# A twelve-stage decoder kernel: the scan stage interleaved over its token groups, with its last norm and the context attention's first queries moved across the stage border

## The reference

```
fg  = sigmoid(h @ W_F)                                  # (tokens, 128)
t   = h @ W_toP + sum_i W_V[:, i] * (h @ W_U[:, :, i])  # four products, i = 0..3
lam = sigmoid(fg @ W_lam);  u = t @ B_mat               # (tokens, 64)
s_n = lam_n * s_(n-1) + u_n                             # a scan along each sequence
x   = x + (t + s @ C_mat) @ W_fromP
```

## Time and profile before

| | |
|---|---|
| median of 3 runs | 2536.81 us (2535.66 to 2538.05) |
| the profiled execution | 2539.63 us |
| its span in the trace | 2537.8 us |
| busy in the span | PE 80%, DVE 58%, ACT 43%, POOL 29% |
| scan stage in the trace | 970.8 to 1066.0 us |
| first score matmul of the context attention | 1075.2 us |

### The profile page before, as it was taken

The page is one execution under the profiler, slowest core; times in us unless marked ns, Lnnn a source line. Parts: engine busy times, 40 slices in busy tenths (PEclk is TensorE's granted clock), DMA queues, the critical chain, the costliest instruction groups (busy, mean ns, idle before and its releaser), DMA issues.

```text
span 2537.8 us, 34717 instructions
## 1 busy us (share of the span) xinstructions
PE 2033.2 (80%) x12069; PEld 1385.2 (55%) x12069; DVE 1482.4 (58%) x4604; ACT 1087.6 (43%) x2654; POOL 748.3 (29%) x755
## 2 busy tenths in 40 slices
PE   4778776989799997488872999857778887998779
PEld 3444444777555563255631678646645456666546
DVE  5655535444475555378740386488767764666662
ACT  2232232544443331078710256667657322666331
POOL 3111123211132230124236155364343332001252
PEclk9899988999899998789975999978989898999789
DMA  2000000200330001100043145600040000000000
GB/s 95 1 0 34 0 34 2 87 26 1 140 118 1 1 1 65 42 18 27 10 175 120 49 138 154 202 1 1 1 169 22 30 1 15 1 1 2 36 1 34
DMA packets 39117, 117.52 MB, mean 46 GB/s; under 512 B 6672, under 2 KB 24208, under 8 KB 36848
## 3 DMA queue, kind: packets, MB, share of 16 engines
q1 hardware_dynamic: 31312, 94.19, 11.1%
q0 software_dynamic: 7632, 21.11, 2.2%
HBM read 92.08 MB, written 36.04 MB: 50 GB/s over the span
## 4 chain that ended last, share of the span: by engine, by line
PE 58%; DVE 18%; ACT 11%; POOL 5%; issue 4%; another core or an unknown queue 3%; DMA 1%; POOLq 0%; DVEq 0%; SPq 0%; ACTq 0%
PE ps L215 37%; PE ps L737 5%; ACT BIG L814 3%; PE ps L709 3%; PE ps L756 3%; PE ps L1771 2%; PE ps L280 2%; DVE XN L271 1%; ACT BIG L290 1%; DVE SML L256 1%; PE ps L1783 1%; PE ps L843 1%; PE ps L1247 1%; POOL SML L221 1%
## 5 line engine op out<-in xcount | busy, mean ns | idle before, releaser
L215 PE MATMUL ps<-BIG 128*128 128x256 f16 (+2 forms) x1616 | 341.7, 361 | 26.4 <-DVE BIG L2339 12.9
L814 ACT ACTIVATE BIG<-BIG,SML 128x256 f32<-128x256 f32 (+1 forms) x768 | 302.5, 483 | 23.8 <-DVE SML L777 23.8
L215 PEld LDWEIGHTS ps<-BIG 128*128 128x128 f16 (+1 forms) x1616 | 223.9, 140 | 121.6 <-issue 66.6
L737 PE MATMUL ps<-CST,BIG 128*128 128x128 f32 x1408 | 217.0, 290 | 41.8 <-ACT BIG L814 26.1
L635 POOL TENSOR_TENSOR BIG<-BIG 128x512 f16<-128x512 f32 x120 | 142.2, 1186 | 293.2 <-ACT BIG L569 264.9
L737 PEld LDWEIGHTS ps<-CST,BIG 128*128 128x128 f32 x1408 | 160.9, 146 | 118.7 <-ACT BIG L814 76.6
L215 PE MATMUL ps<-XN,BIG 128*128 128x512 f16 x864 | 206.8, 396 | 13.8 <-ACT BIG L546 4.9
L219 POOL TENSOR_SCALAR SML<-SML 128x4 f32<-128x4 f32 (+1 forms) x88 | 24.4, 277 | 640.6 <-DVE SML L259 267.7
L777 DVE CUSTOM_DVE_ANT_0 BIG<-ps,BIG 128x256 f32<-128x256 f32 x512 | 181.3, 420 | 51.1 <-PE ps L709 50.6
L290 ACT ACTIVATE BIG<-ps 128x512 f32<-128x512 f32 (+1 forms) x240 | 126.7, 564 | 145.9 <-PE ps L737 108.5
L215 PE MATMUL ps<-XT,WA 128*128 128x256 f32 (+1 forms) x320 | 123.6, 523 | 65.7 <-ACT XN L1988 27.1
(11 more groups left out here) (391 smaller groups left out, 4057.3 us busy)
## 6 DMA issues: line engine op xcount, KB each, us to landing
slots<-in_zeros SPq DMA_DIRECT2D x19, 660.0 KB, 24.0
WA<-slots SPq DMA_DIRECT2D x95, 132.0 KB
BIG<-in_l1e SPq DMA_DIRECT2D x2, 4224.0 KB, 17.2
BIG<-spread SPq DMA_DIRECT2D x16, 512.0 KB, 6.1
BIG<-in_l0e SPq DMA_DIRECT2D x8, 768.0 KB, 7.8
BIG<-in_ctxT SPq DMA_DIRECT2D x8, 512.0 KB, 3.6
BIG<-in_ctxT SPq DMA_DIRECT2D x16, 256.0 KB, 3.1
BIG<-in_ctx SPq DMA_DIRECT2D x16, 256.0 KB, 3.6
```

The costliest lines, as they stand in the source:

```text
L215: m = T.e.matmul(ps, l, r, start=i == 0, stop=i == len(pairs) - 1)
L737: m = T.e.transpose(PS[r][:, o:o + P], c["SM"][n % 2 * 4 + i][:, q, tok(k)], ident)
L814: A.e.activation(s[:, q, 0:kn[q]], s[:, q, 0:kn[q]], ACT.Exp, bias=mx[:, q:q + 1], scale=-1.0).then_inc(*(A.sig("exp", p, n, i) if q else ...
```

## The change

The scan stage is interleaved. PE runs the products of group g with `cs(g-1)` put before the second `up`, the transposes of group g-2 before the third, and `fp(g-1)` between `lam(g)` and `ui(g)`. DVE starts a round with the scan of g-1, and the scaling and copy of group g-2's norm come between its additions; the statistics of g-1 end the round. ACT's and POOL's lists follow. The norm of the last group (3) leaves the scan stage: its statistics, root, scaling, transposes and copies are side work of the context attention, at steps 6, 14 and 16 there and, on POOL, after the mask of the fourth sequence.

The loads of `itok` and of the first two sequences' keys and values are issued at the beginning of the scan stage, ahead of the expert weights that SP loads there. POOL sets the columns of ones, converts `itok`, and makes the queries, mask and values of the first sequence inside the scan stage. For this the scan stage's tiles tT and lam move to the end of RING and ui, sT, FG and TT to the upper part of SCR, and the attention's VA, KB, VR, AM and QB lie in the lower part. The other context attention (phase 7) uses the same functions and keeps its order.

The diff, cut to its core:

```diff
-            return p in (2, 8, 11) and p != phases[0] and g == NG - 1
+            return p in (2, 4, 8, 11) and p != phases[0] and g == NG - 1
...
                     norm_upper(after(p), b // 2)
 
+        def late_dve(p):
+
+            if ends_later(p, NG - 1):
+                norm_stats(p, NG - 1)
+                yield from pause(14)
+                norm_scale(V, p, NG - 1)
+                yield from pause(4)
...
+
+        def late_pe(c):
+            if ends_later(c["p"], NG - 1):
+                yield from pause(18)
...
+        def late_act(p):
+            if ends_later(p, NG - 1):
+                yield from pause(18)
+                norm_copy(A, p, NG - 1, 0)
...
+        def first_kv(c):
             if c["p"] == 4:
                 SP.e.dma_start(c["sq"], a["itok"]).then_inc(*SP.sig("itok", by=16))
...
+            for b in range(2):
+                load_kv(c, b)
+
+        def ctx_sp(c):
+            if c["p"] != 4 or 3 not in phases:
+                first_kv(c)
...
+                waits(G, ("xt", 4, b // 2, 0), ("xt", 4, b // 2, 1))
...
-        def ctx_pool(c):
+        def ctx_ready_pool(c):
             p = c["p"]
             ones_columns(c)
             waits(G, (f"w{p}",), ("ones", p, 0), ("ones", p, 1))
...
-            ctx_mask_pool(c, 0)
...
+        def ctx_pool(c):
+            p = c["p"]
+            begun = p == 4 and 3 in phases
+            if not begun:
+                ctx_ready_pool(c)
+                ctx_mask_pool(c, 0)
...
                     ctx_mask_pool(c, b + 1)
+                if b == 2 and ends_later(p, NG - 1):
+                    norm_root(p, NG - 1)
...
+            get = scratch((9216, SCRN))
+            c = {n: RING[:, 8192 + 2048 * i:10240 + 2048 * i] for i, n in enumerate(("tT", "lam"))}
+            c["ui"], c["sT"] = get(2048), get(2048)
...
+        def input_pe(c, g, name):
+            w, src, ready = {"lam": ("wlam", c["FG"][g % 2], ("fg", g)), "ui": ("bm", c["tT"][:, cut(g)], ("tt", g, 4))}[name]
+            b, before = c["ring"].take((name, g), (name + "c", g))
+            waits(T, *before)
+            waits(T, ready)
+            T.e.matmul(PS[b][0:64, :], W[3][w], src, start=True, stop=True).then_inc(*T.sig(name, g))
+
+        def carry_pe(c, g):
+            b, before = c["ring"].take(("cs", g), ("tout", g))
+            waits(T, *before)
+            waits(T, ("scan", g))
+            T.e.matmul(PS[b], W[3]["cm"][0:64, :], c["sT"][0:64, cut(g)], start=True, stop=True).then_inc(*T.sig("cs", g))
+
+        def result_pe(c, g):
+            T.wait_ge(*at("tout", g))
+            for h in range(2):
+                b, before = c["ring"].take(("fp", g, h), ("xb", 3, g, h))
                 waits(T, *before)
...
+                for i in range(2):
+                    m = T.e.matmul(PS[b][:, i * 256:(i + 1) * 256], c["TT"][g % 2][:, tok(2 * h + i)], W[3]["wfrom"],
+                                   start=True, stop=True)
+                m.then_inc(*T.sig("fp", g, h))
...
+            for g in range(NG):
+                waits(T, ("x16", 3, g))
+                for n, (name, w, i, free) in enumerate([("fgp", "wf", 0, ("fg", g)), ("ttp", "wp", 0, ("tt", g, 0))]
+                                                       + [("up", "wu", i, ("tt", g, i + 1)) for i in range(4)]):
+                    if n == 3 and g:
+                        carry_pe(c, g - 1)
+                    if n == 4 and g >= 2 and after(3) is not None:
+                        norm_turn(R, after(3), g - 2)
+                    b, before = R.take((name, g, i), free)
+                    waits(T, *before)
+                    hi, lo = c["w"][w]
+                    group(PS[b], [x for k in range(2) for x in three(hi[:, k, tok(i)], lo[:, k, tok(i)], k, g)]
+                          ).then_inc(*T.sig(name, g, i))
+                input_pe(c, g, "lam")
...
+                    result_pe(c, g - 1)
+                input_pe(c, g, "ui")
+            carry_pe(c, NG - 1)
+            if after(3) is not None:
+                norm_turn(R, after(3), NG - 2)
+            result_pe(c, NG - 1)
+            if after(3) is not None and not ends_later(after(3), NG - 1):
+                norm_turn(R, after(3), NG - 1)
...
             for g in range(NG + 1):
+                if g:
+                    scan_dve(c, g - 1)
                 if g < NG:
...
+                if g >= 2 and after(3) is not None:
+                    norm_scale(V, after(3), g - 2)
+                if g < NG:
+                    add_up(c, g, 0)
                 if g:
...
                     V.e.tensor_tensor(c["TT"][(g - 1) % 2], tT[:, cut(g - 1)], bank("cs", g - 1), ALU.add).then_inc(
                         *V.sig("tout", g - 1))
+                if g < NG:
+                    add_up(c, g, 1)
+                if g >= 2 and after(3) is not None:
+                    norm_copy(V, after(3), g - 2, 1)
+                if g < NG:
+                    add_up(c, g, 2)
+                    add_up(c, g, 3)
+                if g:
                     for h in range(2):
                         waits(V, ("fp", g - 1, h))
                         xx = X[:, 4 * g - 4 + 2 * h:4 * g - 2 + 2 * h, :].rearrange("p t d -> p (t d)")
                         V.e.tensor_tensor(xx, xx, bank("fp", g - 1, h), ALU.add).then_inc(*V.sig("xb", 3, g - 1, h))
-                if g < NG:
-                    waits(V, ("lamc", g), ("uic", g))
-                    for b in range(2 * g, 2 * g + 2):
-                        sl = slice(b * 256, (b + 1) * 256)
-                        V.e.tensor_tensor_scan(c["sT"][0:64, sl], c["lam"][0:64, sl], c["ui"][0:64, sl], 0.0, ALU.mult,
-                                               ALU.add).then_inc(*(V.sig("scan", g) if b % 2 else V.step()))
-                if g:
-                    finish(tail_dve(after(3), g - 1, ("xb", 3, g - 1, 1)))
+                    if g < NG and after(3) is not None:
+                        norm_stats(after(3), g - 1, ("xb", 3, g - 1, 1))
+            if after(3) is not None and not ends_later(after(3), NG - 1):
+                finish(tail_dve(after(3), NG - 1, ("xb", 3, NG - 1, 1)))
+
...
+                if g >= 2:
+                    finish(tail_act(after(3), g - 2))
+                if g < NG:
...
                     waits(A, ("ui", g))
                     A.e.activation(c["ui"][0:64, cut(g)], bank("ui", g)[0:64, :], ACT.Copy).then_inc(*A.sig("uic", g))
...
         def l1_attn_pool(c):
+            if 4 in phases:
+                ctx_ready_pool(S4)
             for g in range(NG):
-                finish(tail_pool(after(3), g))
+                if after(3) is not None and not ends_later(after(3), g):
+                    norm_root(after(3), g)
+                if g == 0 and 4 in phases:
+                    ctx_mask_pool(S4, 0)
+                    ctx_values_pool(S4, 0)
...
+                    if p == 3 and 4 in phases:
+                        first_kv(S4)
```

More of the change, by code:

```diff
@@ L2158, in l1_attn_pe @@
             waits(T, ("w3",), ("wlo", 3, 0))
-            for g in range(NG + 1):
-                if g < NG:
-                    waits(T, ("x16", 3, g))
-                    for name, w, i, free in ([("fgp", "wf", 0, ("fg", g)), ("ttp", "wp", 0, ("tt", g, 0))]
-                                             + [("up", "wu", i, ("tt", g, i + 1)) for i in range(4)]):
-                        b, before = R.take((name, g, i), free)
-                        waits(T, *before)
-                        hi, lo = c["w"][w]
-                        group(PS[b], [x for k in range(2) for x in three(hi[:, k, tok(i)], lo[:, k, tok(i)], k, g)]
-                              ).then_inc(*T.sig(name, g, i))
-                if g:
-                    b, before = R.take(("cs", g - 1), ("tout", g - 1))
-                    waits(T, *before)
-                    waits(T, ("scan", g - 1))
-                    T.e.matmul(PS[b], W[3]["cm"][0:64, :], c["sT"][0:64, cut(g - 1)], start=True, stop=True).then_inc(
-                        *T.sig("cs", g - 1))
-                    T.wait_ge(*at("tout", g - 1))
-                    for h in range(2):
-                        b, before = R.take(("fp", g - 1, h), ("xb", 3, g - 1, h))
-                        waits(T, *before)
-                        for i in range(2):
-                            m = T.e.matmul(PS[b][:, i * 256:(i + 1) * 256], c["TT"][(g - 1) % 2][:, tok(2 * h + i)],
-                                           W[3]["wfrom"], start=True, stop=True)
-                        m.then_inc(*T.sig("fp", g - 1, h))
-                if g < NG:
-                    inputs_pe(c, g)
-                if g and after(3) is not None:
-                    norm_turn(R, after(3), g - 1)
@@ L2201, in l1_attn_dve @@
                         *V.sig("tt", g, 0))
-                    for i in range(4):
-                        waits(V, ("up", g, i), ("tt", g, i))
-                        V.e.scalar_tensor_tensor(tT[:, cut(g)], bank("up", g, i), c["wva"][:, i:i + 1], tT[:, cut(g)],
```

(5 more changed lines are left out.)

71 lines of the change are left out of this document (38 added, 33 removed).

## The result

The changed kernel takes 2490.99 us (median of 4 runs, 2489.09 to 2492.42) against 2536.76 us before (4 runs): 45.8 us less, ratio 0.9819 with a 95% interval of 0.9802 to 0.9836. The forecast was 2496.6, in a range of 2489 to 2507. So the forecast of 40.2 us less was 5.6 us short of the difference of the medians, and the median lies 2.0 us inside the range's lower end.

What follows compares the result with a forecast made beforehand. The prediction took waits from engine to engine in the scan stage, and the border behind it, as the bound. Terms -41.5 + 2.3 - 1.0 = -40.2 us took the median 2536.81 to 2496.6, range 2489 to 2507.

Steps and rivals of the forecast that it cites:

- What bounds the kernel: Scan stage and the border behind it: set by waits from engine to engine, 6.5 us of PE idle per group.
- A full group: Scan stage: groups cost PE's sum, 12.9, 13.9 and 13.9 us, with slack of 1.1 before cs.
- The tail: Scan stage's end: PE idles 2.8 us, then runs between full and half clock; first scores earlier by a middle of 41.5 us.
- -43.3: First scores' gain in us if the scan stage's tail runs at full clock; at half clock -39.9.
- The border: Between scan stage and first scores: the 9.2 us come back, hidden under PE's 13.9; already counted in the -41.5.
- rival (c): Border: the opening isn't hidden and first scores still wait 9.2 us for POOL or a transfer; 2506 us, chance 0.03.
- What the attention takes back: Context attention: insertions cost 0.1 at step 6, 0.7 at step 14, 1.5 at step 16; sum +2.3 us (1.1 to 6.5).
- The first steps: Start of the attention: steps at half clock, 6.47 against 5.08 us, gain 0 to 4; -1.0 us taken.
- (a): Scan stage: POOL and DVE hold each other up, in mask work and in roots beside scans; 2501 us, chance 0.08.
- (b): Scan stage: the chain stays, PE waits for the scan in each group, up to 19.5 us; 2516 us, chance 0.05.
- (d): Attention: all 32 steps at half clock, 1.39 us more each, 44.5 in all; 2541 us, slower than before, chance 0.02.
- Later stages keep their lengths: Stages behind the attention begin earlier with unchanged lengths; a change of more than 2 us would mean the prediction is wrong.

Runs made afterwards that it cites:

- no_late_norm: The changed kernel with the norm of group 3 back in the scan stage: 2460.45 us against 2493.35 before on that chip, ratio 0.9865.
- opening_alone: The kernel before, old order and last norm kept, with the first sequence's loads, queries, mask and values made inside the scan stage: 2479.66 us, ratio 0.9932.
- no_early_opening: The changed kernel with the first queries, mask and values, and their loads, back at the start of the context attention: 2461.27 us, ratio 0.9860.
- two_late_norms: The changed kernel with the last scan ahead of group 2's statistics and group 2's transposes and copies moved to attention step 9: 2500.57 us, ratio 0.9848.
- delay_9: The changed kernel with nine fills of a dead tile on VectorE ahead of its fence at the scan stage's end: 2498.73 us, ratio 0.9847.
- the last version: As two_late_norms, but with the turn and copies of group 2 at the start of attention step 12 in place of step 9: ratio 0.9831.

## Why the prediction was right, step by step

**What bounds the kernel.** Right: waits from engine to engine in the scan stage, and a transfer at the border. With them gone PE is at 100% there.

**A full group.** 12.9, 13.9 and 13.9 predicted, 13.0, 13.8 and 13.8 measured. The slack of 1.1 at cs is shown by two runs, one that used part of it and one that went beyond it. The transposes ran at full clock.

**The tail.** Predicted 2.8 us of idle time and then something between full and half clock, measured 2.87 and nearly half clock: 11.2 us from the last ui to the first scores where the middle was 9.9 and the half-clock end 11.6. This is the term that was mis-sized, in taking the middle: scan stage and border gave 40.3, not 41.5. The -43.3 was weighed there by the rule of the Trainium skill (TensorE: Matmul & The Clock Gate, section "What's actually happening"). The trace agrees with it on the entry: the granted clock was 1.00 up to the idle time. The -43.3 still didn't come: behind the 2.87 us of idle time most of the work was at half clock, 0.70 over the tail.

**The border.** 9.2 predicted and shown by taking the opening out (9.20). In the changed kernel 0.03 us are left from the stage's end to the first scores, so rival (c) is out.

**What the attention takes back.** Predicted 2.3 (1.1 to 6.5), measured 1.3: 0.1 or less at step 6 for 0.1, 0.47 at step 14 for 0.7, 0.87 ahead of the scores of step 16 for 1.5. The interval there was 5.95 us, below the 6.2 to 7 that the prediction named. Queueing the copies behind the transposes cost nothing beyond the transposes themselves.

**The first steps.** -1.0 predicted, -0.9 measured at step 0. But no_late_norm and opening_alone, which have no idle border either, take 7.3 there like the kernel before; and so does no_early_opening, which has the changed kernel's tail and the idle border. So the missing border alone doesn't give it, and neither does the shorter tail. It comes where the first scores still run at full clock: 1.15 us for them in the changed kernel, 2.12 in no_early_opening. In two_late_norms and delay_9, with a shorter tail and a delayed one, step 0 takes 7.3 again.

**Rivals.** (a) had something true in it. POOL's timeline shows the root beside a scan and without one, in no_late_norm:

```profile
1022.26 0.47 POOL L219 TENSOR_SCALAR SML<-SML 128x4 f32<-128x4 f32 x1 [11.95 <-DVE SML L259]
1022.81 1.31 POOL L221 TENSOR_TENSOR SML<-SML,CST 128x4 f32<-128x4 f32 x1
1033.58 0.19 POOL L219 TENSOR_SCALAR SML<-SML 128x4 f32<-128x4 f32 x1 [9.45 <-DVE SML L259]
1033.85 1.01 POOL L221 TENSOR_TENSOR SML<-SML,CST 128x4 f32<-128x4 f32 x1
```

0.47 + 1.31 beside the scan, 0.19 + 1.01 alone; the scan itself took 1.23 against 1.26 before. In two_late_norms, where the scan of the last group is over, the root of group 2 takes 1.20. The rule of the Trainium skill, SBUF — State Buffer, section "Who interferes with whom", agrees in its direction, since the scan's two inputs are in SBUF and the root reads SBUF; that one stands still for the other's whole length these durations don't show. By these durations it costs up to 0.6 us once, in the tail (an estimate: PE waited 0.46 there for the scaling), and nothing in the groups, where PE was never idle. The price that (a) named, a DVE that stands still for POOL's mask work, didn't show: groups 2 and 3 both took 13.8, and only group 2 has that work. (b) is out by its 1.1 us of slack, (d) by the steps, which got 2.5 shorter in sum. What (d) had against it, that step 4 and later ones run at full clock, wasn't quite so before: steps 6 and 10 took 6.36 and 6.30.

**Later stages keep their lengths.** This sentence of the prediction failed in the profile. The stages behind the attention's steps came out 7.1 us shorter, beyond the 2 us that the prediction had named as a sign of being wrong, and from the scores of step 0 to the end of the span it was 9.6 us shorter (1462.6 to 1453.0), where less than 2 was forecast. The experiments show that single stages change their length from one execution to the next of the same kernel, with no change of code. They don't show that the whole 7.1 us is of this kind.

**How much of the hit is luck.** The local terms as measured, 40.3 + 0.9 - 1.3, make 39.9, beside the 40.2 predicted. That they agree so closely is in part chance: the tail gave 1.2 less than predicted, and the insertions cost 1.0 less. The medians are 45.8 apart in the first runs and 42.0 on chip 12. By the ratios the 39.9 lie outside the first interval (41.6 to 50.2) and inside the second (35.0 to 42.4). So the mechanism and its terms are confirmed by the stage lengths. The totals carry some 2 to 6 us more that the prediction had no term for; 2.8 of them may be step 21, and the cause of the rest is open.

## What to carry to other kernels

When a stage loops over groups and its engines hand work round in a circle, sum each engine's work per group first. Here PE's sum was 12.9 to 13.9 us and DVE's 10.9, every hand-over of the neighbouring group fitted with a microsecond to spare, and the interleaved order reached PE's sum. The spare time could be read from the profile before a line was written. Work at a stage border (a transfer, a mask, a last norm) was worth its full chain length in the stage where it had stood. But a thing moved into the neighbour costs what the host step has no room for: 0.9 us at a plain step, 4.7 at one with a sequence's output transposes behind it. It can also push the work of a third engine, as at step 13 of the last version. Judge such a change by the lengths of the stages it touches in two or more profiles, and the rest by the same kernel run again.

## What the hardware showed that I had not expected

- In two profiles of one kernel an unchanged stage of 1888 matmuls took 242.2 or 246.7 us, with the granted clock at 0.98 or 0.95, and an earlier stage 230.2 or 226.7. Yet the time from the first weight load behind the attention's steps to the end of the span agreed to 0.2 us. The total of the changed kernel ran from 2487.65 to 2500.65 on one chip.
- The kernel before took 2537 to 2538 us in the first runs and on chip 12, and 2490 to 2493 on two other chips. The stretch of the expert tiles in phase 5 took 250 to 252 us in the profiles of the former and 207 to 211 in those of the latter, whichever the kernel; why was not tried. The comparisons hold within a chip.
- GpSimd's root lengthened by half beside a scan on VectorE, from 1.20 to 1.78 us, and the scan did not.
- A fill of 0.48 us on VectorE that the next one waits for came every 0.66 us: 0.17 us lay between two dependent instructions.
